# Three layers of graph attention on one core: small copies move from VectorE to ScalarE, and two subtractions become one

## The reference, cut to what matters

```python
h = jnp.maximum(_layernorm(x, axis=-1), 0.0)
for l in range(NL):                                   # 3 layers
    f_ni, f_nj = nf @ W_ni, nf @ W_nj
    f_out = f_ni[src] + f_nj[dst] + ef @ W_fij + bias
    f_out = leaky_relu(f_out, 0.2).reshape(-1, H, D)
    e = einsum('ehd,hd->eh', f_out, attn)
    a = exp(e - segment_max(e, dst)[dst])
    a = a / segment_sum(a, dst)[dst]
    m = (nf @ W_node).reshape(-1, H, D)[src] * a[:, :, None]
    nf, ef = segment_sum(m, dst).mean(axis=1), f_out.mean(axis=1)
x = x + nf
```

## Time and profile before

| what | value |
|---|---|
| median of 3 runs | 3000.43 us (3000.24 to 3002.9) |
| profiled execution, span | 3006.7 us |
| instructions | 50077 |
| TensorE, VectorE, ScalarE, GpSimd busy | 80%, 83%, 48%, 68% of the span |
| TensorE's granted clock, mean | 0.843 of full speed |
| regular part, layer 0 / 1 / 2 (43 sub-blocks each) | 725 / 724 / 793 us |
| first of these at | 156 / 1104 / 2050 us |

### The profile page before, as it was taken

How to read it: one execution, slowest core, us unless ns; L and a number is a source line. 1 busy time by engine, 2 the same in 40 slices (tenths; PEclk the granted TensorE clock), 3 DMA queues, 4 the chain that set the end, 5 groups by cost and what they waited for, 6 DMA issues and landing times.

```text
span 3006.7 us, 50077 instructions
## 1 busy us (share of the span) xinstructions
PE 2404.8 (80%) x15871; PEld 1878.0 (62%) x16027; DVE 2490.5 (83%) x6428; ACT 1447.6 (48%) x3416; POOL 2058.9 (68%) x2167
## 2 busy tenths in 40 slices
PE   3388888888887378888888887649999888998984
PEld 1366667676764356667766665337777777776753
DVE  7399999999997468998999998637888888879784
ACT  0155555555555135555556555414445454445452
POOL 6777777777770577777777776377776666667653
PEclk9699988888899589987999999857778787778796
DMA  6235454535342324343435342332333343333222
GB/s 252 64 96 156 122 147 116 152 110 158 110 128 85 112 74 142 119 149 110 157 111 158 110 153 98 118 103 67 100 120 99 98 136 98 108 108 100 91 92 81
DMA packets 139275, 353.92 MB, mean 118 GB/s; under 512 B 43895, under 2 KB 96027, under 8 KB 120207
## 3 DMA queue, kind: packets, MB, share of 16 engines
q1 hardware_dynamic: 67216, 296.09, 27.9%
q0 software_dynamic: 68960, 39.71, 8.6%
q10 hardware_dynamic: 2838, 14.91, 1.3%
HBM read 137.79 MB, written 212.77 MB: 117 GB/s over the span
## 4 chain that ended last, share of the span: by engine, by line
PE 39%; DVE 29%; issue 14%; ACT 9%; POOL 5%; DMA 3%; SPq 1%; DVEq 0%; ACTq 0%; POOLq 0%
DVE U L1349 12%; PE f_ps L695 12%; PE pick_ps L664 10%; PE f_ps L704 9%; PE xT_ps L685 5%; DVE rows L1266 4%; DVE lr L1277 4%; DVE U L1334 3%; POOL rows L554 2%; ACT f_low L850 2%; ACT xT L841 2%; ACT up L901 2%; PE f_ps L714 2%; ACT wide_ps L889 1%; DVE rows L1378 1%
## 5 line engine op out<-in xcount | busy, mean ns | idle before, releaser
L554 POOL DMA_INDIRECT rows<-nf_tab,src_sb x1995 | 1889.3, 947 | 706.9 <-issue 574.9
L704 PEld LDWEIGHTS f_ps<-w_out,lr 128*128 128x128 f32 x4836 | 701.0, 210 | 379.0 <-issue 277.3
L664 PE MATMUL pick_ps<-nf_part,z 125*128 125x160 bf16 x6345 | 630.0, 264 | 258.4 <-issue 217.0
L1349 DVE TENSOR_TENSOR_SCAN U<-wide_ps,U 128x272 f32<-128x272 f32 (+2 forms) x1272 | 801.6, 694 | 3.2 <-ACT wide_ps L889 2.4
L695 PE MATMUL f_ps<-xT,w_edge 97*128 97x512 f32 x1212 | 753.8, 708 | 22.6 <-ACT ef_new L872 12.0
L664 PEld LDWEIGHTS pick_ps<-nf_part,z 125*128 125x128 bf16 x6345 | 564.6, 112 | 289.8 <-issue 241.3
L704 PE MATMUL f_ps<-w_out,lr 128*128 128x36 f32 (+1 forms) x4836 | 649.8, 274 | 31.2 <-DVE lr L1277 28.8
L1277 DVE TENSOR_TENSOR lr<-f_ps,f_low 128x512 f32<-128x512 f32 x606 | 410.0, 677 | 252.4 <-ACT f_low L850 247.0
L850 ACT ACTIVATE f_low<-f_ps 128x512 f32<-128x512 f32 x606 | 361.0, 596 | 495.9 <-PE f_ps L695 495.9
L685 PE MATMUL xT_ps<-ident,rows 128*97 128x128 f32 x2418 | 431.8, 305 | 76.8 <-issue 37.2
L841 ACT ACTIVATE xT<-xT_ps 97x512 f32<-97x512 f32 x606 | 358.8, 592 | 147.8 <-PE xT_ps L685 145.6
(11 more groups left out here) (163 smaller groups left out, 1070.5 us busy)
## 6 DMA issues: line engine op xcount, KB each, us to landing
u_tab<-up SPq DMA_DIRECT2D x144, 1088.0 KB
s_nd<-edge_first SPq DMA_DIRECT2D x48, 768.0 KB
rows<-nf_tab,src_sb POOLq DMA_INDIRECT x1995, 2.5
ef_tab<-ef_new SPq DMA_DIRECT2D x32, 768.0 KB
ef_st<-ef_tab SPq DMA_DIRECT2D x32, 768.0 KB
z<-fifth_tab SPq DMA_DIRECT2D x141, 96.0 KB
edge_first<-s_nd ACTq DMA_DIRECT2D x16, 768.0 KB
ef_st<-in_edge_attr_dram SPq DMA_DIRECT2D x16, 672.0 KB
```

The lines of the kernel that those rows point to most:

```text
L554: eng.indirect_dma_start(rows[q % RING][:, c * K:c * K + D], None, nf_tab[:, :], bass.IndirectOffsetOnAxis(ap=src_sb[:, t:t + 1], axis=0)) ...
L664: mm = eng.matmul(pick_ps[:, i * PB:(i + 1) * PB], hot[m % 2][0:NQ, f * PW + i * P:f * PW + (i + 1) * P], nf_part[a][0:NQ, f * PB:(f + 1) ...
L704: mm = eng.matmul(f_ps[n % 2][:, u * m:(u + 1) * m], lr[y][:, u * P:(u + 1) * P], w_out[l][:, 0:m], start=True, stop=True)
L1349: last = eng.tensor_tensor_scan(uh[:, c0 * w:c1 * w], dbc[h % 2][:, 0:(c1 - c0) * w], uh[:, c0 * w:c1 * w], 0.0, ALU.mult, ALU.add)
```

## The change

It has three parts.

1. The copy of the carried sums (L1327) leaves VectorE. ScalarE does it in a new step `carry(k)`, once for each sub-block but the first of a layer: in the regular loop ahead of `lay_out` in slot i = 1, elsewhere behind `widen`. VectorE's waits ahead of `product` for the sums of the previous sub-block go with it.
2. The write of the first fifth (L1374) leaves VectorE. ScalarE does it in `take_picks(b)`, in slot i = 2 behind L864 and L872, and two at the start of a layer.
3. The tiles `mx` and `sc` become two halves of one tile, and so do `e_dec` and `e_wt`. Decay and weight exponents come from one subtraction of 128 elements a partition, in place of two of 64. The weight exponents have thereby one column more for each head than before. `weigh` waits for this subtraction alone, and `widen` of head 0 for the addition of the cuts.

```diff
-        mx = [sb(f"mx{s}", [P, H * W1]) for s in range(2)]
+        HW1 = H * W1
+        mx_sc = [sb(f"mx_sc{s}", [P, 2 * HW1 + 2]) for s in range(2)]
+        mx = [a[:, 0:HW1] for a in mx_sc]
+        sc = [a[:, HW1:2 * HW1] for a in mx_sc]
...
-        sc = [sb(f"sc{s}", [P, H * W1]) for s in range(2)]
-        e_dec = [sb(f"e_dec{s}", [P, H * W1]) for s in range(2)]
-        e_wt = [sb(f"e_wt{s}", [P, H * SB]) for s in range(2)]
+        e_dw = [sb(f"e_dw{s}", [P, 2 * HW1]) for s in range(2)]
+        e_dec = [a[:, 0:HW1] for a in e_dw]
+        e_wt = [a[:, HW1:2 * HW1] for a in e_dw]
...
                     def weigh(k):
-                        n = H * sub_w(k % NB)
-                        eng.wait_ge(expo_done, k * 3 + 3)
+                        w = sub_w(k % NB)
+                        eng.wait_ge(expo_done, k * 2 + 1)
...
+                    def carry(k):
+                        w, before = sub_w(k % NB), sub_w(k % NB - 1)
+                        eng.wait_ge(sums_done, H * k)
+                        eng.activation(carry_of(U[k % 2], w)[:, :, 0, :],
+                                       carry_of(U[1 - k % 2], before)[:, :, before, :],
+                                       ACT.Copy).then_inc(carried, 1)
+
+                    def take_picks(b):
+                        m = l * NPICK + b
+                        q = l * NS + b * SB // SUP
+                        eng.wait_ge(pick_ready, PICK * (m + 1))
+                        if q >= RING:
+                            eng.wait_ge(turned, groups_to(q - RING))
+                            eng.wait_ge(prod_done, subs_to(q - RING))
+                        eng.activation(picked_rows(q, b), pick4[:, :, 0, :], ACT.Copy
+                                       ).then_inc(picked, 1)
...
                     def widen(k, h):
                         if 4 * k + h >= 2:
                             eng.wait_ge(sums_done, 4 * k + h - 1)
+                        if h == 0:
+                            eng.wait_ge(expo_done, k * 2 + 2)
...
                         if i == 1 and g >= 2 * GB:
+                            carry(k)
                             lay_out(k - 1)
+                        if g >= 0 and i == PICK - 1 and g // GB + 2 < NPICK:
+                            take_picks(g // GB + 2)
...
-                        eng.tensor_tensor(ed3[:, :, 1:w + 1], mx3[:, :, 0:w],
-                                          mx3[:, :, 1:w + 1], ALU.subtract
-                                          ).then_inc(expo_done, 1)
-                        eng.tensor_tensor(e_wt[s][:, 0:w * H].rearrange("p (h t) -> p h t", h=H),
-                                          sc3[:, :, 1:w + 1],
-                                          mx3[:, :, 1:w + 1], ALU.subtract
-                                          ).then_inc(expo_done, 1)
-                        eng.wait_ge(expo_done, 3 * k + 1)
+                        both = [P, 2, H, w]
+                        eng.tensor_tensor(
+                            e_dw[s][:, :].rearrange("p (a x) -> p a x", a=2)[:, :, 0:n]
+                            .rearrange("p a (h t) -> p a h t", h=H)[:, :, :, 1:w + 1],
+                            mx_sc[s][:, :].rearrange("p (a x) -> p a x", a=2)[:, :, 0:n]
+                            .rearrange("p a (h t) -> p a h t", h=H)[:, :, :, 0:w],
+                            wide(mx[s][:, 0:n].rearrange("p (o h t) -> p o h t", o=1, h=H)
+                                 [:, :, :, 1:w + 1], both),
+                            ALU.subtract).then_inc(expo_done, 1)
+                        eng.wait_ge(expo_done, 2 * k + 1)
...
-                        if k:
-                            eng.wait_ge(sums_done, H * k)
                         if k >= 2:
                             eng.wait_ge(up_ready, 2 * k - 2)
-                        if b:
-                            eng.tensor_copy(u4[:, :, 0, :], carry_of(U[1 - s], before)[:, :, before, :]
-                                            ).then_inc(carried, 1)
-                        else:
+                        if b == 0:
                             eng.memset(u4[:, :, 0, :], 0.0).then_inc(carried, 1)
...
-                        eng.wait_ge(pick_ready, PICK * (m + 1))
+                        to = picked_rows(q0 + b * SB // SUP, b)
                         eng.wait_ge(fifth_ready, 9)
-                        if q >= RING:
-                            eng.wait_ge(turned, groups_to(q - RING))
-                            eng.wait_ge(prod_done, subs_to(q - RING))
-                        to = rows3[q % RING][:, c:c + GT * (PICK - 1) + 1:GT, 0:D]
-                        eng.tensor_copy(to, pick4[:, :, 0, :]).then_inc(picked, 1)
```

More of the change, by code:

```diff
@@ L351, in rows_sem_to, with picked_rows @@
                             if (v % NS) * GS + a < NG)
+        def picked_rows(q, b):
+            c = b * SB % SUP + 2
+            return rows3[q % RING][:, c:c + GT * (PICK - 1) + 1:GT, 0:D]
         def carry_of(u, w):
@@ L876, in weigh @@
                     def weigh(k):
-                        n = H * sub_w(k % NB)
-                        eng.wait_ge(expo_done, k * 3 + 3)
+                        w = sub_w(k % NB)
+                        eng.wait_ge(expo_done, k * 2 + 1)
                         if k:
                             eng.wait_ge(sums_done, 4 * k - 1)
-                        eng.activation(wts[:, 0:n].rearrange("p (t h) -> p t h", h=H),
-                                       e_wt[k % 2][:, 0:n].rearrange("p (h t) -> p t h", h=H),
+                        eng.activation(wts[:, 0:H * w].rearrange("p (t h) -> p t h", h=H),
+                                       by_head(e_wt[k % 2], w)[:, :, 1:w + 1]
+                                       .rearrange("p h t -> p t h"),
                                        ACT.Exp).then_inc(wt_ready, 1)
+                    def carry(k):
[13 more added lines that the diff above has]
+                                       ).then_inc(picked, 1)
                     def widen(k, h):
@@ L910, in _ @@
                     put_ef(0)
+                    take_picks(0)
+                    take_picks(1)
                     kl = l * NB - 1
@@ L1015, in _ @@
                     widen(k + 1, 0)
+                    carry(k + 1)
                     lay_out(k)
@@ L1232, in slice_b @@
                             eng.wait_ge(dst_spread, (q - 1) * D)
-                            eng.wait_ge(expo_done, 3 * subs_to(q - 2))
+                            eng.wait_ge(expo_done, 2 * subs_to(q - 2))
                         eng.tensor_copy(same_b[q % 2][:, 0:w], same[:, s * SUP:s * SUP + w]
@@ L1319, in product @@
                         r = (q0 + sup) % RING
-                        before = sub_w(b - 1)
                         u4 = carry_of(U[s], w)
-                        if k:
-                            eng.wait_ge(sums_done, H * k)
                         if k >= 2:
                             eng.wait_ge(up_ready, 2 * k - 2)
-                        if b:
-                            eng.tensor_copy(u4[:, :, 0, :], carry_of(U[1 - s], before)[:, :, before, :]
-                                            ).then_inc(carried, 1)
-                        else:
+                        if b == 0:
                             eng.memset(u4[:, :, 0, :], 0.0).then_inc(carried, 1)
```

2 lines of the change are left out of this document (removed).

## The result

The changed kernel takes 2903.9 us (median of 4 runs, 2899.5 to 2908.6), beside 3001.7 for the kernel before: ratio 0.9655, 95% interval 0.9619 to 0.9691. The forecast was 2952, its range ended at 2905. So the sign was right, the size was half of what came, and the case that came nearest is rival (a), the clock that gives back much (2911). The kernel before itself varied from one comparison to the next (medians 2998 to 3018), so each experiment is judged by its ratio to the runs beside it.

What follows compares the result with a forecast made beforehand. VectorE sets the pace at full clock, 16.3 us a sub-block, with low-clock stretches of TensorE above it and GpSimd near. VectorE's 35 us plus the clock's 14 make 49, 3000.4 to 2951, say 2952; range 2905 to 2998.

Steps and rivals of the forecast that it cites:

- rival (a): TensorE's clock gives back much: 40% of 136 us, 54, with 35 makes 89; time about 2911; chance 0.21.
- VectorE's terms: VectorE's sub-blocks: 0.14 + 0.26 - 0.06 = 0.34 us with scans, 0 without, 0.23 each at full clock; 35 us in all.
- bounds of 0.44 lost and 0.2 won: Sub-block without scans, paced by ScalarE's chain: 0 taken, between 0.44 us lost and 0.2 us won.
- the clock term: TensorE's clock: of 136 us lost to the lower level, a tenth comes back, 14 us; -40 to +60 kept open.
- the 60 that I kept open: TensorE's clock: the forecast fails as a whole if the clock's share moves by more than 60 us.
- Rival (b): ScalarE's chain takes the gain: carry and first write delay `lower`, 16 us left, time 2984; chance 0.17.
- Rival (c): Slower: carry ahead of L872 lengthens a second TensorE idle time, 28 more clock falls cost +24, time 3025; chance 0.13.
- Rival (d): No change: GpSimd or a locked rhythm of the clock keeps the pace, near 3000; chance 0.05.
- GpSimd's bound of 26 us for layer 1: Regular part of layer 1: GpSimd's 13 gathers take 16.2 us a sub-block, so it can't gain more than about 26 us.
- a measurement can tell 6 us from no change: Whole kernel: a measurement can tell 0.2%, 6 us, from no change; chance of landing within that 0.07.
- the signs: Signs of being right include 0.29 us subtraction, no idle time before first predicated copy, TensorE's wait before fetch near 1.3 us.
- VectorE's busy sum: VectorE: busy sum down by some 95 us from the removed copies and second subtraction, the span by less.

Runs made afterwards that it cites:

- e7: The changed kernel with ScalarE's carry moved from slot 1 to behind `take_scores` of slot 2; 2898.8 us, ratio 0.9664.
- e10: The changed kernel with four unread matmuls on TensorE ahead of the turn (four transposes) of the slot in which a fetch begins; 2874.2 us.
- e9: The kernel before with four unread matmuls on TensorE ahead of the turn (four transposes) of the slot in which a fetch begins; 2895.8 us.
- e4: The changed kernel with the same two copies also done on VectorE, into a tile nobody reads; 2952.2 us, ratio 0.9788.
- e11: e7 (carry one slot later) with four unread matmuls ahead of the turn; 2869.5 us, ratio 0.9554.
- e3: The kernel before with only the shared tiles and one subtraction, both copies left on VectorE; 2995.9 us, ratio 0.9941.

## Where the prediction was right, and where it failed

- **VectorE's terms** (0.14 carry, 0.26 first write, 0.06 back for the subtraction; 35 us) were right as a pace, partly by luck: 0.27 us a sub-block at full clock, forecast 0.23. Two errors cancelled: a sub-block with scans gained 0.49 and 0.59, not 0.34, and the one without scans lost 0.26, not 0. I had given that one bounds of 0.44 lost and 0.2 won and took 0. The carry in ScalarE's chain made most of the loss (0.21 by e7). As microseconds of the whole kernel the 35 were not reached: e10 against e9 gives 22, and 12 of them in the regular parts. TensorE waits more for GpSimd's rows there, in layer 1 and partly in layer 2; that this takes the rest is argued, not tested.
- **The step that failed is the clock term**: "I take a tenth, 14 us". It measured 68 us by the pace, half of the 137 that lay above the full-clock pace, and 91 by the kernels with filling. Both are above the 60 that I kept open, beyond which, by my own sign, the forecast fails as a whole. I had reasoned that the idle time doesn't vanish but only moves. It does move (the waits of the unused matmuls for `ef_new` went from 53.9 to 94.7 us), but the falls don't go by the sum: there are 42 in place of 88. In layers 0 and 1 of the kernel before, the clock fell behind 20 of 27 waits above 2.2 us and behind all 18 of 1.3 to 1.5; in the changed kernel the longest waits, now 1.8 to 2.0, were followed by falls 6 times in 14, and only 2 of 1.3 to 1.5 are left. I priced by the share of idle time that goes what has to be priced by the number of falls that go. Why so many go in layer 2 (41 before, 25 now) stays open: e4 has 29 there at the old length of VectorE's work.
- **Rival (a)** was right that the falls go; its 40% was low (68 of 137 are 50%). The objection to it, that the longest waits stay near 1.9 us, was true, but fewer falls followed them.
- **Rival (b)**: ScalarE's chain took 0.26 in one sub-block of three and no more. **Rival (c)**, slower by the second idle time: that wait did grow (from 0.71 to 0.87 us at full clock), and the falls became fewer all the same. A slip in its sum: half of 43 falls is 22, net +11 us; the 28 falls that it prices give the +24. **Rival (d)** in part: by e10 against e9, layer 1 has nothing to gain with the clock held up, and TensorE waits there for GpSimd's rows.
- GpSimd's bound of 26 us for layer 1 held: that part shrank by 16.
- That a measurement can tell 6 us from no change was too hopeful: over the comparisons the kernel before ran from 2990 to 3028 us.
- Of the signs, the subtraction of 0.29 us, the predicated copies without idle time in front, and a mean wait ahead of a fetch of 1.34 us (166.5 / 124) were there. VectorE's busy sum fell by 55 us, not 95: the sum counts time in which two instructions overlap once, and I had taken the full lengths of copies of which a part lay under the next instruction.

The Trainium skill ("TensorE: Matmul & The Clock Gate", A second HAM failure mode: psum-queue depth-cycling) tells of a kernel in which short idle times between groups of matmuls make the clock swing between its two levels and cost throughput. The traces here agree, with waits of 1.2 to 2.4 us, and e9 puts the price at about 100 us of 3000 in this kernel.

## What to carry to other kernels

Before pricing an edit on the engine that sets the pace, split the span into full-clock and low-clock stretches and ask at which of TensorE's waits the clock falls. Shortening such waits can be worth more than their length (here 51 us less of waiting ahead of the fetches in the regular parts, and 68 to 91 us by the clock), and the same gain was had without touching the other engines, by unread matmuls ahead of the wait. Put them where they wait for nothing of their own and where nothing urgent stands behind them: the same four matmuls gave -102 us ahead of the turn and +90 us behind a wait for ScalarE. Compare two edits with the clock held up in both (e10 against e9), or the clock's rhythm is measured along with the edit; and look at more than one execution before laying a layer's time to an edit.

## What the runs showed of the hardware

- The lower level (1.2 GHz) came with idle times as short as 1.0 to 1.3 us in a third of the cases (77 of 233), in an engine that is 78 to 80% busy. With 0.87 us of matmuls ahead of the turn (e9, 407.41 to 408.28), waits of the same length were followed by no fall in 34 cases (e9 to e11): what the engine did before the wait counts too, not the wait alone.
- The falls lock into patterns that repeat over three sub-blocks (layer 2 of e4). One program varies with them from execution to execution: the kernel before by 39 us (2990 to 3028, over all comparisons), e3 by 43 (2971 to 3015, nine of its ten runs), and the ones with free filling by 5 to 16, in four runs each.
- A copy of 132 scattered elements on ScalarE lasts 0.33 us, but its successor starts 0.20 after it; one of 96 elements lasts 0.31 with the successor 0.13 behind.
